# One walk over twelve tiles in the expert stage, keys projected before x's norm, four groups' key stacks issued by ScalarE

## The reference

```python
x = x + attention(_layernorm(x), ctx, ctx)          # 16 heads, d_k 16, softmax
y = _layernorm(x)                                   # per token, over 256
x_norm = y * rsqrt(mean(y*y) + EPS) * norm_w
q = (x_norm @ wq).reshape(B, T, 8, 2, 128)
sim = einsum('bthpd,hkpd->pbthk', q, keys)          # 8 heads x 2 halves x 64 keys
s1, i1 = top_k(sim[0], 16);  s2, i2 = top_k(sim[1], 16)
all_scores = s1[..., :, None] + s2[..., None, :]    # 256 sums
final_scores, pk = top_k(all_scores, 16)            # 16 of 4096 experts per head
hidden = gelu(einsum('btd,bthkd->bthk', x_norm, expert_down[final_idx]))
out = einsum('bthk,bthkd->btd', hidden * relu(final_scores), expert_up[final_idx])
x = x + out
```

## Time and profile before

| | us |
|---|---|
| median of 3 runs | 1132.27 (1129.2 to 1135.19) |
| profiled execution, its own time | 1135.81 |
| its span in the trace | 1134.0 |
| PE busy | 1025.6 (90%) |
| DVE busy | 884.4 (78%) |
| POOL busy | 628.1 (55%) |
| ACT busy | 395.0 (35%) |
| share of PE in the chain that ended last | 68% |

### The profile page before, as it was taken

How to read it: one execution, slowest core, us unless ns; L and a number is a source line. 1 busy time by engine, 2 the same in 40 slices (tenths; PEclk the granted TensorE clock), 3 DMA queues, 4 the chain that set the end, 5 groups by cost and what they waited for, 6 DMA issues and landing times.

```text
span 1134.0 us, 27487 instructions
## 1 busy us (share of the span) xinstructions
PE 1025.6 (90%) x10088; PEld 724.9 (64%) x10088; DVE 884.4 (78%) x4242; ACT 395.0 (35%) x741; POOL 628.1 (55%) x790
## 2 busy tenths in 40 slices
PE   5899979987887875799999999999999999999998
PEld 3434344333233235678888788788788788788887
DVE  3776556998998987999988988988989889734110
ACT  2366645544553642222222222222222222222211
POOL 5330520441123127878788778867876887777411
PEclk9699989988897996799999999999999999999999
DMA  7544224222121125200000000000000000010000
GB/s 205 140 131 150 92 78 145 88 89 91 52 68 34 49 103 197 101 6 23 22 22 22 22 22 22 16 23 28 16 23 27 16 23 27 11 32 2 1 19 10
DMA packets 60342, 63.78 MB, mean 56 GB/s; under 512 B 7184, under 2 KB 56592, under 8 KB 59696
## 3 DMA queue, kind: packets, MB, share of 16 engines
q1 hardware_dynamic: 59728, 61.63, 17.1%
q10 hardware_dynamic: 480, 0.39, 0.2%
HBM read 42.34 MB, written 19.66 MB: 55 GB/s over the span
## 4 chain that ended last, share of the span: by engine, by line
PE 68%; DVE 17%; POOL 5%; issue 5%; ACT 2%; DMA 1%; SPq 1%; ACTq 0%; POOLq 0%; DVEq 0%; another core or an unknown queue 0%
PE bank L1434 65%; DVE mem L1340 5%; PE bank L1437 3%; DVE mem L1389 2%; POOL mem L870 1%; DVE mem L1186 1%; DVE mem L1185 1%; POOL mem L731 1%; ACT mem L997 1%; DVE mem L1182 1%; DVE mem L1190 1%; POOL mem L877 1%; DVE mem L1205 1%; DMA parts_d<-mem 1%; DVE mem L1194 1%
## 5 line engine op out<-in xcount | busy, mean ns | idle before, releaser
L1434 PE MATMUL bank<-mem 128*128 128x32 bf16 (+6 forms) x9608 | 979.0, 274 | 67.0 <-DVE mem L1340 13.6
L1434 PEld LDWEIGHTS bank<-mem 128*128 128x128 bf16 (+4 forms) x9608 | 672.4, 123 | 325.5 <-issue 124.1
L870 POOL TENSOR_TENSOR mem<-mem 128x1536 bf16<-128x1536 bf16 x121 | 333.4, 2762 | 93.5 <-DVE mem L1384 53.1
L1340 DVE TENSOR_REDUCE mem<-bank 128x1 f32<-128x512 f32 x256 | 166.1, 682 | 55.6 <-PE bank L1434 55.1
L997 ACT ACTIVATE mem<-bank 128x512 f32<-128x512 f32 x256 | 147.8, 602 | 154.5 <-PE bank L1434 153.6
L1389 DVE TENSOR_TENSOR mem<-mem,bank 128x2048 bf16<-128x2048 bf16 x128 | 155.0, 1212 | 54.7 <-PE bank L1434 54.4
L1052 ACT COPY mem<-bank 128x512 f32<-128x512 f32 x128 | 75.1, 586 | 104.8 <-PE bank L1434 104.8
L877 POOL TENSOR_TENSOR mem<-mem 128x512 f32<-128x512 f32 x64 | 81.4, 1271 | 50.9 <-ACT mem L1041 50.9
L1437 PE MATMUL bank<-mem 128*128 128x128 f32 (+3 forms) x480 | 74.7, 287 | 38.0 <-DVE mem L1118 15.6
L1437 PEld LDWEIGHTS bank<-mem 128*128 128x128 f32 (+3 forms) x480 | 55.5, 141 | 80.1 <-issue 55.3
L1043 ACT ACTIVATE bank<-bank 128x512 f32<-128x512 f32 x64 | 37.2, 582 | 180.5 <-PE bank L1434 180.5
(11 more groups left out here) (109 smaller groups left out, 720.2 us busy)
## 6 DMA issues: line engine op xcount, KB each, us to landing
mem<-parts_d SPq DMA_DIRECT2D x186, 64.0 KB, 2.3
parts_d<-mem SPq DMA_DIRECT2D x16, 384.0 KB, 2.9
mem<-in_L_ffn_expert_down SPq DMA_DIRECT2D x16, 256.0 KB, 2.9
downT_d<-mem SPq DMA_DIRECT2D x16, 256.0 KB, 3.1
mem<-downT_d SPq DMA_DIRECT2D x4, 1024.0 KB, 8.4
mem<-in_L_ffn_expert_up SPq DMA_DIRECT2D x4, 1024.0 KB, 12.0
tok_d<-mem SPq DMA_DIRECT2D x16, 160.0 KB, 1.8
mem<-tok_d SPq DMA_DIRECT2D x16, 160.0 KB, 2.2
```

Source lines behind the costliest of these rows:

```text
L870: nc.gpsimd.tensor_tensor(ow[q % 2], i0, i1, ALU.mult).then_inc(ow_rdy, 1)
L1340: nc.vector.tensor_reduce(nmx[g % 2][:, i % TB, i // TB:i // TB + 1], psum[n % 3][:, :], AX.X, ALU.max, negate=True).then_inc(s_max, 1)
L1434: return nc.tensor.matmul(o, l, r, start=first, stop=last)
```

## The change

- **The walk.** There is one walk of ten slots over all twelve tiles. The first three tasks stand where they stood; the other 201 are spread over 98 steps (before: 65 over 32 steps, then 136 over 64). The last task is at step 1 of slot 6 (before: step 15 of slot 5). Tile 16 is neither fetched nor multiplied. The counters of the steps on DVE are reset once per tile, on POOL before each `numbers`.
- **Candidate sums.** The second half's sums move from the step behind the eighth search into the step of that search.
- **`take_out`** moves to the head of ACT's step 2, ahead of the gelu.
- **Second norm.** `mve` and the scale exist twice, `second_norm(b-1, 0)` moves from step 13 to 15, `second_norm(b-1, 1)` from step 15 to step 2 of the next group, and the waits between the halves reach one half further back.
- **Start.** The context is transposed and the first key projection made before x's transposes; DVE splits projections 1 and 0, POOL 3 and 2 (before: DVE 1 and 3, POOL 0 and 2). SP stores these parts and issues the query stacks of groups 0 and 1 around `load_x(1)`; the rest of the loads come behind.
- **Key stacks.** ACT issues the key stacks of groups 0 to 3, SP only the query stacks.

```diff
-        before = [(0, "xT", (0, 0)), (0, "xT", (0, 1)), (0, "cT", (0, 0)), (0, "cT", (0, 1)), (0, "proj", (0, 0)),
-                  (0, "proj", (0, 1)), (0, "proj", (0, 2)), (0, "proj", (0, 3)), (0, "v", (0, 0)), (0, "v", (0, 1))]
+        before = [(0, "cT", (0, 0)), (0, "cT", (0, 1)), (0, "proj", (0, 1)), (0, "xT", (0, 0)), (0, "xT", (0, 1)),
+                  (0, "proj", (0, 0)), (0, "proj", (0, 3)), (0, "proj", (0, 2)), (0, "v", (0, 0)), (0, "v", (0, 1))]
...
+            n = (TILES - NA) * len(TASKS)
+            tasks = [(11 + 5 * t // FEW if t < FEW else 16 + 98 * (t - FEW) // (n - FEW),
+                      NA + t // len(TASKS), *TASKS[t % len(TASKS)]) for t in range(n)]
+            for x in range(16 * 10):
...
+                       "mult": [(tile + 1, x - s) for s, tile, kind, i in tasks
+                                if x - s in (0, 1) and (kind, i) == ("extract", 0) and tile + 1 < TILES],
-                       "sums": [(t0 + t, 2 * i // FH) for s, t, kind, i in tasks if s + 1 == x and kind == "search" and
-                                2 * (i + 1) % FH == 0],
+                       "sums": [(tile, 2 * i // FH) for s, tile, kind, i in tasks
+                                if kind == "search" and (s + 1, i) in ((x, FH // 2 - 1), (x + 1, FH - 1))],
...
             load_setup(0)
+            store_parts(0, 1)
+            store_parts(0, 0)
+            load_stacks(0, ("q",))
             load_x(1)
+            load_stacks(1, ("q",))
             load_setup(1)
+            store_parts(0, 3)
+            store_parts(0, 2)
             load_weight(3, Wo, o_ld)
...
                 if g < 2:
-                    load_stacks(g + 2)
+                    load_stacks(g + 2, ("q",))
...
+            def load_keys(g):
+                act.wait_ge(part_wr[1 + 2 * (g // 2)], 16)
+                for s in range(NSLOT):
+                    dst, src = stack(g, "k", s)
+                    nc.scalar.dma_start(dst, src).then_inc(st_ld[g], 16)
             for _, name, index in before:
                 take(name, index)
-                if (name, index) == ("proj", (0, 3)):
...
+                if (name, index) == ("proj", (0, 0)):
+                    load_keys(0)
+            load_keys(1)
...
+                    if i == 8 and g < 2:
+                        load_keys(g + 2)
...
-                for q, k, par, kk, now in walk(*where):
+                for q, k, par, kk, now in walk():
+                    if q == 2 and on(kk, 1, 8):
+                        take_out(k)
                     if on(kk, 0, 7):
                         gelu(k * 16 + q, q)
...
-                    if q == 2 and on(kk, 1, 8):
-                        take_out(k)
...
-                    if r == 2 and b >= 1 and i in (13, 15):
-                        second_norm(b - 1, (i - 13) // 2)
+                    if b >= 1 and (r, i) in ((2, 15), (3, 2)):
+                        second_norm(b - 1, r - 2)
```

More of the change, by code:

```diff
@@ L162, in build @@
         st6e = mem.take(CH * 6).rearrange("p (t c) -> p t c", t=CH)
-        mve = mem.take(CH * 2).rearrange("p (t c) -> p t c", t=CH)
-        chain = [mem.take(CH) for _ in range(6)]
+        mve = [mem.take(CH * 2).rearrange("p (t c) -> p t c", t=CH) for _ in range(2)]
+        chain = [mem.take(CH) for _ in range(5)]
+        scale2 = [mem.take(CH) for _ in range(2)]
         mem.at = mark
@@ L415, in restart @@
                     self.n = 0
[L420 to L425, removed]
         def on(k, lo, hi):
-            return k is None or lo <= k <= hi
+            return lo <= k <= hi
         FEW = 3
[L433 to L449, removed]
-                       "sums": [(t0 + t, 2 * i // FH) for s, t, kind, i in tasks if s + 1 == x and kind == "search" and
-                                2 * (i + 1) % FH == 0],
[L452 to L455, removed]
@@ new lines, in walk @@
+        def walk():
+            n = (TILES - NA) * len(TASKS)
+            tasks = [(11 + 5 * t // FEW if t < FEW else 16 + 98 * (t - FEW) // (n - FEW),
+                      NA + t // len(TASKS), *TASKS[t % len(TASKS)]) for t in range(n)]
+            turned = NA - 1
+            for x in range(16 * 10):
+                now = {"tasks": [(tile, kind, i) for s, tile, kind, i in tasks if s == x],
+                       "fetch": [tile + 1 for s, tile, kind, i in tasks
+                                 if s == x and (kind, i) == ("search", 4) and tile + 1 < TILES],
+                       "mult": [(tile + 1, x - s) for s, tile, kind, i in tasks
+                                if x - s in (0, 1) and (kind, i) == ("extract", 0) and tile + 1 < TILES],
+                       "sums": [(tile, 2 * i // FH) for s, tile, kind, i in tasks
+                                if kind == "search" and (s + 1, i) in ((x, FH // 2 - 1), (x + 1, FH - 1))],
+                       "numbers": [tile for s, tile, kind, i in tasks if s + 1 == x and (kind, i) == ("choose", 0)],
+                       "turn": [tile for s, tile, kind, i in tasks if s + 3 == x and (kind, i) == ("extract", 3)]}
@@ L878, in weigh_hidden, with run @@
                   .then_inc(m_pool, 1)
-            def run(*where):
-                for q, k, par, kk, now in walk(*where):
+            def run():
+                for q, k, par, kk, now in walk():
                     if on(kk, -1, 6) and (k + 1) * 16 + q not in OWN:
@@ L895, in run @@
                             weight_parts(tile)
-                steps.restart()
-            runs(pool, run)
+            run()
         @block.scalar
@@ L1080, in run @@
                         take_sim(tile, n)
-            runs(act, run)
+            run()
         @block.vector
@@ L1421, in run @@
                         weigh_hidden(k1, p1, q1)
-                    for task in now["tasks"]:
-                        choose_experts(*task)
+                    for tile, kind, n in now["tasks"]:
+                        if (kind, n) == ("search", 0):
+                            steps.restart()
+                        choose_experts(tile, kind, n)
                     if q == 4 and on(kk, 1, 8):
                         add_residual(k)
-                steps.restart()
-            runs(dve, run)
+            run()
         @block.tensor
```

72 lines of the change are left out of this document (31 added, 41 removed).

## The result

| | before | after |
|---|---|---|
| median of 4 runs, us | 1132.49 (1129.2 to 1135.19) | 1095.16 (1093.21 to 1096.84) |
| ratio | | 0.9665, 95% interval 0.9641 to 0.9688 |
| span of the profiled execution, us | 1134.0 | 1093.3 |
| mean granted clock of PE, as a share of 2.4 GHz | 0.944 | 0.964 |

The time came out 37.3 us lower; 1093 was predicted. The spans differ by 40.7, because the profiled execution of before stood above its median. In the changed kernel the lines shift: L1434 is L1425, L1437 is L1428, L1340 is L1330, L1403 is L1393, L1057 is L1047, L1201 is L1191, L731 is L714, L870 is L854, L1161 is L1151, L804 is L788, and L1013 is L995, now ACT's issue of four groups' key stacks. In some kernels of the experiments the lines stand one or two off from these.

The account below looks back on a forecast made before the run. PE was taken as the bound, held up by waits on DVE and ACT, with DVE setting the pace in attention groups 8 to 15. The terms sum to -39.1: 1135.8 to 1096.7, less 3.5 gives 1093; range 1087 to 1101.

Parts of the forecast that it names:

- take_out: Expert stage, head of ACT's step 2: seven PE waits of 1.17 us on the output copy go, -8.2; lower end 4.
- Candidate sums and the spread: Expert stage: DVE's 3.15 us wait for POOL's sums goes, four slots reach slot 1's length, -18.4; lower end 0.
- the price of the spread: Expert stage: keys and first extract share a step in tiles 10, 11, 14; four waits of 1 us, +4, ends 0, 12.
- Tile 16: Expert stage: its similarities no longer cost PE half of 7.5 us, -3.5; ends 0 and 3.7.
- Second norm: Attention stage: DVE's six waits for POOL's scale, 13.7 us, go; -10.5 taken, ends 3 and 18.
- the upper end: Second norm's end of 18: all 13.7 us of DVE waits and some 4 us of half-speed PE after three of them.
- Start: Start of the kernel: first scores at about 28.6 us against 31.19, -2.5 taken; ends +2 and -5.
- The condition: Start, key stacks: moving DMA issue is worth nothing unless SP's order is waited for; no gain in the sum.
- DVE is not the bound in the slots: Judges the expert-stage rival that DVE stays the bound and waits on L1403 move to other steps: 1108, chance 0.14.
- POOL's order: Expert-stage rival: sums ahead of the weighing wait for DVE's eighth search, 6 us per tile, 48 us, 1141; chance 0.03.
- more clock: Rival: without pauses PE stays at full speed in the start and groups 6 to 15, another 8 us, 1085; chance 0.10.
- the start gives nothing: Rival: key stacks on ACT hold other projections, second batch late, first scores gain nothing, 1096 to 1098; chance 0.04.

Follow-up runs that it names:

- the three pairs: Kernel before against changed kernel (1132.49, 1095.16 us); kernel before against it with the second norm's part alone (1118.93); second norm's place put back (1111.89) against changed kernel.
- both kernels with late sums: Changed kernel with the second half's candidate sums one step later again, 1101.18 us; the same with the old task density too, 1114.67 us.
- the norm alone: Kernel before with only the second norm's part of the change (doubled statistics and scale, both halves moved): 1118.93 us, ratio 0.9859.
- sums late with old density: Changed kernel with the second half's candidate sums one step later and the old task density (65 over 32 steps, 136 over 64): 1114.67 us, ratio 0.9829.

## Why the prediction was right

Measured in differences of the two traces and the experiments, by its own steps:

- *take_out*, -8.2: 8.1 with it put back. Right for this kernel, but only since the sums are early; with the old stall in place it and tile 16 together bring 6.6, not the 11.5 of the two terms.
- *Candidate sums and the spread*, -18.4, with *the price of the spread*, +4, -14.4 in all: slots 2 to 5 are 23.4 us shorter, of which 4.6 is the wait for `take_out`'s copy and 3.4 tile 16, which leaves 15.4; slot 1 is 1.3 longer than 83.66; in the whole stretch 23.6 - 8.1 - 3.4 = 12.1. The price is 4.2 us in the slots where 4 was put. Its reason was half right: one wait for a key (1.86), but at tile 7, which I hadn't named, and behind a wait for POOL's numbers; none at tiles 10, 11 and 14; and two for the numbers in bank 1, which I hadn't seen. DVE's slack in a slot is 2.4 us (81.4 of 83.8), less than the 3 to 6 that I put. What failed is the credit: the thin rate of slot 1 was taken for part of the cure, and with early sums it is only a cost.
- *Tile 16*, -3.5: slot 5 shows 3.4.
- *Second norm*, -10.5: mis-sized. It is some 15 to 17 us. I counted DVE's waits and took the clock into the upper end alone; the windows show that 12.0 of the 17.1 us are PE's own work done at a higher clock, and 5.0 less idle time (8.8 to 13.3 and 4.3 to 5.7 in the three pairs).
- *Start*, -2.5: right up to the first scores, nothing after them. I had priced ACT's eighteen issues at nothing, because "its evictions in groups 0 and 1 wait for PE or POOL", and had not added that the issue also waits for the store ahead of it, while the next eviction stands behind. That is PE's wait of 4.96.

The sum was -39.1 and the two profiled executions differ by 40.7: -6.6 too little for the norm, +2.4 too much for the start and +2.5 for the stretch nearly cancel, so part of the match is luck.

DVE's split in the start took 2.34 us and not 3.5, with both casts at 0.43: POOL's split comes only later, at 22.07. By the rule in the Trainium skill, SBUF — State Buffer, section Who interferes with whom, it would be 0.8 less. The trace agrees and shows 1.1 less, 0.8 of it in the second cast (1.26 to 0.43) and 0.3 in the first subtraction (0.98 before, 0.69 now). The 0.45 of the first cast before wasn't alone, as the prediction has it: an operation of POOL's ran until 18.90 beside it. The first scores came 3.0 earlier, between the 2.5 without that rule and the 4 with it. The gain does not reach the end, because of ACT.

The condition set beside the rule of the Trainium skill, DMA: Bandwidth & Descriptors, section Issuing engines are not separate DMA queues, was that SP's order is what is waited for. The trace with stacks 2 and 3 on SP meets it: PE stands 5.42 us behind SP's order, and moving the issues does pay, 1093.07 against 1097.38, once they stand at steps where no PE wait for ACT follows.

The rivals: DVE is not the bound in the slots; POOL's order costs nothing (it waited 1.03 us for tile 9's eighth search, and both kernels with late sums are slower); more clock is what happened, in the attention stage; the start gives nothing, as its rival said, though by ACT's eviction in group 0 and not by late first scores.

## What to carry to other kernels

Two changes that cure the same stall don't add, and one of them may cost once the other is in: take each back alone and both together. Price the removal of a pause by the clock as well, from one window over the stage with the same instructions. And when an issue of DMAs is moved to another engine, ask what it has to wait for there and which eviction stands behind it: here the wrong step on ACT cost about as much as the move gained.

## What the runs showed of the hardware

- In the attention stage the same 1412 to 1415 matmuls took 273.0 us of PE at a granted clock of 0.96 and 285.1 at 0.91. In three pairs of kernels that differ in DVE's six waits of 2.2 to 2.3 us on average, or in more, the clock's part of the gain was 8.8 to 13.3 us and the idle time's 4.3 to 5.7.
- PE's seven waits of 1.16 us, one per slot, leave its clock at 1.00 (slot 1 of before), and so do single waits of 1.86 and 1.94 (slot 1 of after and with late sums). Twelve slots have a wait of 2.06 to 2.27 (before, the norm alone, and sums late with old density): eleven show 0.98, and one, with waits of 1.63 and 2.25, 1.00. So the length of the wait alone does not tell.
- A cast of 128x512 from f32 to bf16 on DVE took 0.43 us where POOL did nothing and 1.26 in one place beside POOL's split; the first one there took 0.45 beside POOL too.
- Executions scatter by some 3 us in the attention stage and at the start, in kernels that are alike there (313.4 to 316.1, and 79.2 to 82.5 for the average of group 0), while a slot of the expert stage repeats to 0.05 us. Effects of 1 us can be read from slots, and not from the start.
